# Masked attention scores moved from their PSUM bank into the SBUF ring, exponentials taken in place

## What is computed

```
scores = (Q @ K^T) * scale + mask        # 100 x 361
attn   = softmax(scores, axis=-1)
out    = attn @ V
```

## Time and profile before

| | |
|---|---|
| median of three runs | 1224.86 us |
| the profiled execution: its time, its span | 1225.07 us, 1223.3 us |
| PE busy, share of the span | 1150.0 us, 94% |
| PEld (weight loads) | 944.6 us, 77% |
| DVE | 801.3 us, 66% |
| ACT | 766.9 us, 63% |
| POOL | 251.5 us, 21% |
| granted TensorE clock, mean | 0.99 of full |

### The profile page before, as it was taken

One profiled execution on the slowest core, in us unless ns is written; L12 is line 12 of the kernel. 1 busy time (PEld: TensorE's weight loads), 2 busy tenths in 40 slices (PEclk: granted clock), 3 DMA queues, 4 the chain that ended last, 5 costly groups with the idle time before them and its releaser, 6 DMA issues.

```text
span 1223.3 us, 32246 instructions
## 1 busy us (share of the span) xinstructions
PE 1150.0 (94%) x10003; PEld 944.6 (77%) x10003; DVE 801.3 (66%) x2370; ACT 766.9 (63%) x2179; POOL 251.5 (21%) x264
## 2 busy tenths in 40 slices
PE   4899999999999999999999999999999999999997
PEld 4678787787878778787887878788787878878786
DVE  4455676757576676757667675766767576675735
ACT  3374756757485674748568474866847476584744
POOL 1041212111131211113121121312122131211210
PEclk9799999999999999999999999999999999999999
DMA  7664536547363653726366472635647263564500
GB/s 235 178 178 103 147 86 154 131 101 185 74 161 87 140 144 89 196 70 165 89 132 152 89 184 72 167 95 123 158 92 178 71 159 100 125 166 94 136 14 8
DMA packets 77965, 153.77 MB, mean 126 GB/s; under 512 B 10528, under 2 KB 47200, under 8 KB 77296
## 3 DMA queue, kind: packets, MB, share of 16 engines
q1 hardware_dynamic: 77936, 153.40, 51.7%
HBM read 113.72 MB, written 39.65 MB: 125 GB/s over the span
## 4 chain that ended last, share of the span: by engine, by line
PE 74%; ACT 10%; issue 8%; DVE 5%; DMA 1%; ACTq 1%; DVEq 1%; POOL 1%; SPq 0%; POOLq 0%
PE TP L416 16%; PE PJ L365 15%; PE OA L436 6%; PE SCO L402 6%; PE SCO L682 5%; PE SCO L460 5%; PE PJ L468 5%; PE PJ L378 4%; ACT PT L1058 4%; ACT PR L1047 4%; PE SCO L365 2%; DVE SCO L819 2%; PE SCO L406 2%; PE OA L441 2%; DVE PT L829 1%
## 5 line engine op out<-in xcount | busy, mean ns | idle before, releaser
L819 DVE CUSTOM_DVE_ANT_0 SCO<-SCO,MK 100x361 f32<-100x361 f32 x768 | 405.0, 548 | 173.6 <-PE SCO L402 146.7
L1047 ACT ACTIVATE PR<-SCO,MN 100x361 f32<-100x361 f32 x768 | 427.7, 567 | 140.7 <-DVE MN L819 135.9
L416 PEld LDWEIGHTS TP<-ident,PR 100*128 100x128 f32 x2304 | 223.6, 141 | 103.1 <-ACT PT L1058 57.1
L416 PE MATMUL TP<-ident,PR 100*128 100x100 f32 x2304 | 270.4, 253 | 23.6 <-ACT PT L1058 11.8
L1058 ACT ACTIVATE PT<-TP 121x600 f32<-121x600 f32 x256 | 172.3, 673 | 48.6 <-PE TP L416 48.5
L402 PE MATMUL SCO<-K0S,Q0S 128*100 128x362 f32 x512 | 155.8, 370 | 18.9 <-ACT PR L1047 13.8
L1047 ACT ACTIVATION_READ_ACCUMULATOR PR<-SCO,MN 100x1 f32 x768 | 158.3, 206 | 0.0
L829 DVE COPY PT<-TP 121x600 f32<-121x600 f32 x128 | 99.9, 781 | 20.6 <-PE TP L416 19.3
L1216 POOL TENSOR_TENSOR K1F<-K1F,KB 128x364 f32<-128x364 f32 x64 | 50.7, 793 | 287.7 <-DVE K1F L811 287.7
L819 DVE DVE_READ_ACCUMULATOR2_ANT MN<- 100x1 f32 x768 | 109.5, 143 | 0.0
L402 PEld LDWEIGHTS SCO<-K0S,Q0S 128*100 128x100 f32 x512 | 73.0, 167 | 36.8 <-ACT PR L1047 27.0
(11 more groups left out here) (140 smaller groups left out, 1816.8 us busy)
## 6 DMA issues: line engine op xcount, KB each, us to landing
K1S<-k_scr SPq DMA_DIRECT2D x128, 364.0 KB, 6.4
k_scr<-K1HL SPq DMA_DIRECT2D x64, 364.0 KB, 2.7
Q0S<-q_scr SPq DMA_DIRECT2D x128, 100.0 KB, 4.1
K0S<-k_scr SPq DMA_DIRECT2D x64, 182.0 KB, 5.1
AT<-ctx_cols SPq DMA_DIRECT2D x16, 722.0 KB, 9.2
V<-ctx_rows SPq DMA_DIRECT2D x16, 484.0 KB
q_scr<-QHL SPq DMA_DIRECT2D x16, 400.0 KB, 2.5
k_scr<-K1HL SPq DMA_DIRECT2D x32, 182.0 KB, 3.0
```

The source lines that it names most:

```text
L416: last = pe.transpose(TP[:, k % 2, c * T:(c + 1) * T], PR[0:T, k % NPR, c * SP:c * SP + P], ident[0:T, 0:T])
L819: dve.tensor_tensor_reduce(out=bank, in0=bank, in1=mask[0:T, :], scale=scale, scalar=3.4e38, op0=ALU.add, op1=ALU.min, accum_out=MN[0:T, k ...
L1047: act.activation(PR[0:T, k % NPR, 0:S], SCO[0:T, k % 3, 0:S], ACT.Exp, bias=MN[0:T, k:k + 1], scale=-1.0, accum_out=SM[0:T, k:k + 1]).then ...
```

## The change

The shift writes the masked scores to the ring `PR` in SBUF and not back to their PSUM bank. The exponential is then taken in `PR`, in place. A score now waits for `shifted` of head k-3 and not for `prob`. The wait for the ring buffer (`pt_mm`) moves from the exponential on ScalarE to the shift on VectorE. VectorE waits once, ahead of the first batch, for the GpSimd memset of the ring (`pool_zero`).

```diff
--- before.py
+++ after.py
@@ -586,7 +586,7 @@
                     for k in (2 * p, 2 * p + 1):
                         if k >= 3 or not first:
-                            pe.wait_ge(prob, NH * b + k - 2)
+                            pe.wait_ge(shifted, NH * b + k - 2)
                         score(b, k)
@@ -643,7 +643,7 @@
                 if more:
-                    pe.wait_ge(prob, NH * b + 32)
+                    pe.wait_ge(shifted, NH * b + 32)
                     pe.wait_ge(ct_l2, 2 * b + 4)
                     keys0(range(6))
@@ -713,7 +713,7 @@
                     if p > 17:
-                        pe.wait_ge(prob, NH * b + 2 * p - 2)
+                        pe.wait_ge(shifted, NH * b + 2 * p - 2)
                     score(b, 2 * p)
@@ -727,7 +727,7 @@
                     if p > 16:
-                        pe.wait_ge(prob, NH * b + 2 * p - 1)
+                        pe.wait_ge(shifted, NH * b + 2 * p - 1)
@@ -813,10 +813,11 @@
             def shift(b, k):
 
                 dve.wait_ge(scored, NH * b + k + 1)
+                wait_from(dve, pt_mm, NPAIR * b + k // 2 - 2)
                 dve.sem_inc(met_dve, 1)
-                bank = SCO[0:T, k % 3, 0:S]
                 mask, scale = (MK0, -1.0) if k < 32 else (MK1, -SCALE1)
-                dve.tensor_tensor_reduce(out=bank, in0=bank, in1=mask[0:T, :], scale=scale, scalar=3.4e38,
+                dve.tensor_tensor_reduce(out=PR[0:T, k % NPR, 0:S], in0=SCO[0:T, k % 3, 0:S], in1=mask[0:T, :],
+                                         scale=scale, scalar=3.4e38,
                                          op0=ALU.add, op1=ALU.min, accum_out=MN[0:T, k:k + 1]).then_inc(shifted, 1)
@@ -905,6 +906,8 @@
                         .then_inc(wv_c, 1)
+
+            dve.wait_ge(pool_zero, 3)
 
             def batch(b, first, more):
@@ -1043,8 +1046,7 @@
             def exps(b, k):
                 act.wait_ge(shifted, NH * b + k + 1)
-                wait_from(act, pt_mm, NPAIR * b + k // 2 - 2)
-                act.activation(PR[0:T, k % NPR, 0:S], SCO[0:T, k % 3, 0:S], ACT.Exp, bias=MN[0:T, k:k + 1],
+                act.activation(PR[0:T, k % NPR, 0:S], PR[0:T, k % NPR, 0:S], ACT.Exp, bias=MN[0:T, k:k + 1],
                                scale=-1.0, accum_out=SM[0:T, k:k + 1]).then_inc(prob, 1)
```

## The result

| | before | after |
|---|---|---|
| median, runs of one session side by side | 1224.88 us (4 runs) | 1266.98 us (4 runs, 1266.05 to 1269.14) |
| ratio, 95% interval | | 1.035 [1.033, 1.037] |
| span of the profiled execution | 1223.3 us | 1265.9 us |
| granted TensorE clock, mean | 0.99 | 0.97 |

A forecast was written before the change was run, and what follows sets the result against it. It took the chain shift, exponential, ScalarE's copy, transposes as the bound, not score banks. Terms of +0.35 us a batch over 15 turns, +5.3 us, less 0.5 us, gave +4.8 us: 1229.9 us, range 1215 to 1239 us.

The forecast's parts named there:

- it is an instruction more in the queue: VectorE's shift: the moved ring wait adds a 0.09 us sequencer step, showing where the shift stands idle for its score.
- The number of instructions is the same: TensorE: its waits only change their semaphore, so no instruction is added there.
- The sign: Whole kernel: slower, 1229.9 us, with chance 0.54 for slower.
- score waits gone: TensorE: nothing booked in the 14 steady batches, only the first and last batch gain, -0.5 us in all.
- ring's wait on VectorE: Five shifts a batch that stand idle for their score (33, 0, 4, 8, 26): +0.45 us a batch.
- ring's wait gone from ScalarE: Exponentials 40, 44, 0 and 26, on the chain with ScalarE idle: -0.36 us a batch.
- SBUF for PSUM, exponentials and shifts: On the chain: 14 exponentials at +31 ns make +0.43 us a batch, 11 shifts at -15 ns make -0.17 us.
- All four places: Score waits of a steady batch, together 2.05 us: transposes behind each wait for ScalarE's copy, so earlier scores gain nothing.
- The wait at 408.62: First of the four score waits: score 0.60 us earlier, transposes behind then wait 1.0 us in place of 0.40.
- The score's early start: Rival, TensorE sets the time at some score wait: 0.51 us a batch per place, 1222 us; all four 1187 us; chance 0.26.
- The costs vanish too: Rival: exponentials hide their longer read and the two queue steps balance, 1223 to 1227 us; chance 0.20.
- The merged waits drop the clock: Rival: TensorE waits merging to 1.34 us ahead of 434.41 lower its clock, +22 us, 1252 us; chance 0.03.

The follow-up runs named there:

- Run 2: Changed kernel with 80 idle semaphore increments on VectorE ahead of the first batch, so the loop lies in two code blocks: 1226.69 us, ratio 1.0016.
- run 5: Kernel before the change with 10 idle semaphore increments on VectorE ahead of its first batch: 1224.83 us, ratio 0.9999.
- run 6: Kernel before the change with 22 idle semaphore increments on VectorE ahead of its first batch: 1253.57 us, ratio 1.023.
- run 7: Kernel before the change plus only the ring's wait in VectorE's shift, with 10 idle increments (loop touches a third code block): 1252.75 us, ratio 1.022.
- run 9: Changed kernel without the ring's wait on VectorE, its in-loop scores waiting for `prob` again instead of `shifted`: 1220.67 us, ratio 0.9975.
- run 3: Changed kernel without the ring's wait in VectorE's shift: 1219.81 us, ratio 0.9952.
- 8: Kernel before the change plus only the ring's wait in VectorE's shift, with 80 idle increments (loop in two code blocks): 1232.88 us, ratio 1.0065.
- 11: Changed kernel with 80 idle increments, the ring's wait put ahead of the wait for the score in VectorE's shift: 1219.06 us, ratio 0.9956.
- run 10: Kernel before the change without the ring's wait on ScalarE's exponentials: 1220.36 us, ratio 0.9967.
- run 4: Changed kernel with 12 useless matmuls to an idle score bank in slot 0 of each batch from the second on: 1261.65 us, ratio 1.030.

## Why the prediction was wrong

- **The failed step** is "it is an instruction more in the queue", priced at 0.04 + 0.05 us where the score had arrived. The price was right and it was not the whole price. Nothing in the working counted how many instructions the added wait puts into a written-out loop body (17), or asked where the body's code would lie. "The number of instructions is the same" was said of TensorE, where it was true and beside the point. The prediction's range had no case for code loading: 40.3 us of the 42.1 us. Run 2 shows that it is the place of the code and not the work of the 17 instructions, runs 5 and 6 that the place alone does it, run 7 that this wait does it in the kernel before.
- **The sign was luck.** Slower was forecast from terms of a few us; none of the 40.3 us comes from them.
- **The rest of the sum.** With the stall gone, the change costs 2.0 us by the medians of one session, [0.6, 3.2] by the ratio, where I had +4.8. By terms (a few tenths of an us of each are noise):

| term | predicted | measured |
|---|---|---|
| score waits gone | -0.5 | -0.9, at most -3 (run 9) |
| ring's wait on VectorE | +6.8 | +6.9, +7.2, +7.6 (runs 2 and 3, 8, 2 and 11) |
| ring's wait gone from ScalarE | -5.4 | -3.6 (run 10) |
| SBUF for PSUM, exponentials and shifts | +3.9 | +0.3 (run 9 over run 10) |

- **Mis-sized: SBUF for PSUM.** Exponentials took 591 ns where I had 598, and shifts 530 where I had 533. What I did not see is what follows the shift. Its accumulator read took 82 ns, not 143. This is the way from one shift to its exponential, the same head of a batch, timelines of DVE and ACT, run 10 first:

```profile
426.86 0.53 DVE L819 CUSTOM_DVE_ANT_0 SCO<-SCO,MK 100x361 f32<-100x361 f32 x1
```

```profile
427.48 0.56 ACT L1046 ACTIVATE PR<-SCO,MN 100x361 f32<-100x361 f32 x1 [0.49 <-DVE MN L819]
```

and of run 3:

```profile
424.64 0.52 DVE L818 CUSTOM_DVE_ANT_0 PR<-SCO,MK 100x361 f32<-100x361 f32 x1
```

```profile
425.20 0.60 ACT L1048 ACTIVATE PR<-PR,MN 100x361 f32<-100x361 f32 x1 [0.45 <-DVE MN L818]
```

0.62 us became 0.56, by as much as the accumulator read is shorter (61 ns), while the exponential is 24 ns longer: I had the cost and not the gain. Four such links a batch, 15 x 4 x 0.06, make 3.6 us. That this pays for the whole difference of 3.6 us is argued from these lines; no run has the shift's output moved alone. The trace's 31 ns for copies was above the 24 ns that the exponentials show. So were the 43 ns of the Trainium skill, "VectorE: DVE Perf Modes", section "The TRN2 errata".
- **Right: the score waits.** All four places behaved as read. The wait at 408.62 was to turn the transposes' 0.40 us into 1.0, and it is 0.91 in runs 2 and 3; 0.67 + 0.67 were to merge into 1.34, and it is 1.40. What was not as read is where the waits went. I had all 42.5 us go to the waits for ScalarE's copy, 57.1 to some 100 us. In run 3 these are 80.2 us; those for VectorE's copy went from 14.8 to 20.7 us and those for exponentials from 5.2 to 12.8 us, together 36.6 us more.
- **A slip in the rival's sum.** One place was priced at 7.7 us, and four of them are 31 us, 1199 us; the 1187 us for "all four" is the forecast less all 42.5 us of score waits. No run came near either.
- **The rivals.** The score's early start (0.26) is excluded at its price. "The costs vanish too" (0.20) is what the kernel without the stall does (1226.69 us, in its 1223 to 1227), but not for the reason given: the queue's steps do not balance (+6.9 and -3.6 us), and the longer exponentials are paid for elsewhere, by the argument above by the accumulator reads. "The merged waits drop the clock" (0.03) gave 1252 us, the nearest of all, and was wrong in its mechanism: in run 2 the merged wait of 1.41 us is there and the clock stays up.

```profile
430.00:435.50 5.50, 4.38 (x72) 3.35 (x64) 4.20 (x14) 4.59 (x15) 1.55 (x2) 1.00 0.67 203
435.50:439.00 3.50, 3.50 (x25) 3.07 (x26) 1.17 (x5) 2.93 (x9) 0.00 (x0) 1.00 0.63 223
```

In the changed kernel the clock falls behind the stall, and with TensorE busy through the stall (run 4) it does not. A low stretch of 3.3 us cost 0.62 us, not the half of 3 us that I had taken from the earlier trace rows: part of the slowness went into waits that were there anyway (the transposes at 436.12 wait 0.37 us for ScalarE's copy, and 0.67 us in run 4 with the full clock).

## What to carry to other kernels

Count the instructions of a loop body per engine, those for register values and semaphores included, before and after an edit, and look at the page's queue of instructions: packets in proportion to the loop's turns, and "issue" ahead of the first operation of a turn, mean that the loop no longer fits where it lies. A wait that never holds still costs its step on the engine that runs it last, and where its value depends on the loop's counter it costs code; leave it out where another engine's order implies it, or put it ahead of the wait that is late. And a wait that the profile charges to the busiest engine is worth nothing where the next wait of the same engine hangs on another chain: 42.5 us here bought some 1 us, and 3 at most.

## What the runs showed of the hardware that I had not expected

- A VectorE loop body of 299 to 316 instructions costs 0.30 to 0.36 us at its jump, or 2.8 to 3.9 us, by its place alone. In the one kernel with its start 21 instructions ahead of a boundary there is a second stall, of 2.4 to 5.4 us, at that boundary in 12 of 13 turns; with 39 and 50 ahead there is none. Two blocks of 256 fit every run here.
- The jump takes 3.6 us or more at one instruction behind the boundary, and 2.8 to 3.5 us at 3 to 21. Of the two instruction packets near a jump the second starts 1.0 to 1.3 us behind it in all four kernels that stall, over all their jumps. The first comes with the boundary: 0.6 us behind the jump at one instruction, 0.2 to 0.5 at three, 0.1 at nine, and 3.3 us ahead of it at 21. That the fetch of the third block, still under way, delays that of the loop's start would fit this; no run tries it.
- Only VectorE stalled. TensorE's loop body has 720 instructions in the trace, and its jump takes 0.03 us in all kernels. The Trainium skill, "Runtime: NRT & Kernel Launch", section "Instruction fetch mechanics", gives TensorE room for 2048 instructions, which would explain it. No run here puts TensorE's body over that size.
- VectorE's operation with an accumulator takes 548 ns with its output in PSUM and 530 in SBUF, the read of the accumulator 143 and 82 ns. ScalarE's exponential takes 567 ns from PSUM and 591 from SBUF, and the read behind it 206 and 189 ns.
- How much of a late VectorE reaches TensorE can be read from the traces. From the last shift of a turn to the first instruction of the next it takes 0.44 to 0.46 us in the kernels without the stall, and in the batches shown 4.10 us in the changed kernel, 3.43 in run 6 and 3.18 in run 7: 3.7, 3.0 and 2.7 us late. The transposes behind it waited 2.38, 1.65 and 1.41 us, each time 1.3 us less; in run 2 they don't wait at all, so 1.3 us is their slack. The clock does the rest: over the whole run it was at the low level for 69.4 us in the changed kernel and 27.6 in run 2, 45.6 us in run 6 and 21.9 in run 5, so the stall brought some 42 us of it in the one and 24 in the other. Both go the way of the difference between the 40.3 us that the stall costs in the changed kernel and the 28.7 us of run 6.
